# A third bank for the scores at the end of an attention kernel, and its last maxima one slot earlier

## What is computed

```python
x_n = _group_norm(x, gn_w, gn_b)
q, k, v = to_heads(conv1x1(x_n, wq, bq)), ...        # 4 images, 4 heads, 1024 pixels, 64
attn = jnp.einsum('bhqd,bhkd->bhqk', q, k) * scale
attn = jax.nn.softmax(attn, axis=-1)
out = jnp.einsum('bhqk,bhkd->bhqd', attn, v)
return x + conv1x1(out, wp, bp)
```

## Time and profile before

| | |
|---|---|
| median of 3 runs | 367.43 us (366.38 to 367.86) |
| the profiled execution's own time | 366.56 us |
| its span, first to last instruction | 364.8 us |
| mean granted TensorE clock | 0.998 |
| PE busy | 348.0 us, 95% |
| ACT busy | 303.1 us, 83% |
| DVE busy | 284.0 us, 78% |
| POOL busy | 284.2 us, 78% |

### The profile page before, as it was taken

The page is one execution under the profiler, slowest core; times in us unless marked ns, Lnnn a source line. Parts: engine busy times, 40 slices in busy tenths (PEclk is TensorE's granted clock), DMA queues, the critical chain, the costliest instruction groups (busy, mean ns, idle before and its releaser), DMA issues.

```text
span 364.8 us, 11244 instructions
## 1 busy us (share of the span) xinstructions
PE 348.0 (95%) x4577; PEld 208.6 (57%) x4577; DVE 284.0 (78%) x447; ACT 303.1 (83%) x362; POOL 284.2 (78%) x258
## 2 busy tenths in 40 slices
PE   0899999999999999999999999999999999999996
PEld 0544565655656556655666556565656556655564
DVE  5788899878887787778887777777877787787474
ACT  1748879898877999989878999998889888888982
POOL 5066888699788997998778997998879797967722
PEclk9999999999999999999999999999999999999999
DMA  6055141213743341143553241031552441070113
GB/s 212 19 146 144 45 97 38 30 62 103 135 142 74 80 98 43 24 112 116 124 154 66 60 106 64 10 80 43 117 164 53 94 85 65 2 202 3 31 31 118
DMA packets 38587, 30.92 MB, mean 85 GB/s; under 512 B 23676, under 2 KB 31368, under 8 KB 38536
## 3 DMA queue, kind: packets, MB, share of 16 engines
q1 hardware_dynamic: 37792, 29.15, 32.6%
q10 hardware_dynamic: 744, 1.06, 0.8%
HBM read 9.44 MB, written 4.19 MB: 37 GB/s over the span
## 4 chain that ended last, share of the span: by engine, by line
PE 85%; DVE 8%; ACT 2%; issue 2%; DMA 1%; DVEq 1%; ACTq 0%
PE gen L617 19%; PE st L743 14%; PE st L744 14%; PE pv L766 9%; PE pv L769 8%; PE pv L768 7%; PE st L709 5%; PE mx L709 3%; DVE mx L1053 3%; DVE p_lo L1086 2%; ACT st L969 1%; DVE mx L1049 1%; PE st L617 1%; PE mx L824 1%; DMA xin<-in_x_dram 1%
## 5 line engine op out<-in xcount | busy, mean ns | idle before, releaser
L964 ACT ACTIVATE p_hi<-st 128x1024 f16<-128x1024 f32 x127 | 130.7, 1029 | 40.2 <-PE st L744 38.8
L1328 POOL TENSOR_TENSOR p_lo<-p,p_hi 128x1024 f16<-128x1024 f32 x62 | 132.3, 2133 | 10.4 <-ACT p L969 10.4
L766 PEld LDWEIGHTS pv<-v_hi,p_hi 128*128 128x128 f16 x1024 | 93.4, 97 | 26.7 <-issue 15.0
L766 PE MATMUL pv<-v_hi,p_hi 128*128 128x65 f16 x1024 | 106.4, 195 | 0.3 <-DVE o L1094 0.2
L768 PE MATMUL pv<-v_lo,p_hi 128*128 128x64 f16 x1024 | 105.9, 193 | 0.0
L769 PE MATMUL pv<-v_hi,p_lo 128*128 128x65 f16 x1024 | 105.7, 194 | 0.0
L1086 DVE TENSOR_TENSOR p_lo<-st,p_hi 128x512 f16<-128x512 f32 x126 | 80.8, 683 | 30.0 <-ACT st L969 29.7
L743 PE MATMUL st<-q_twice,k_both 128*128 128x512 f16 x256 | 97.0, 379 | 1.6 <-DVE p_lo L1086 1.2
L768 PEld LDWEIGHTS pv<-v_lo,p_hi 128*128 128x128 f16 x1024 | 93.8, 98 | 6.2
L744 PE MATMUL st<-q_max,k_one 65*128 65x512 f16 x256 | 97.3, 380 | 0.0
L769 PEld LDWEIGHTS pv<-v_hi,p_lo 128*128 128x128 f16 x1024 | 93.9, 97 | 0.0
(11 more groups left out here) (200 smaller groups left out, 558.4 us busy)
## 6 DMA issues: line engine op xcount, KB each, us to landing
q_twice<-st_hi_q SPq DMA_DIRECT2D x64, 64.0 KB, 2.1
xres<-in_x_dram SPq DMA_DIRECT2D x4, 1024.0 KB, 5.2
out_dram<-y SPq DMA_DIRECT2D x13, 256.0 KB, 2.3
xin<-in_x_dram SPq DMA_DIRECT2D x6, 512.0 KB, 4.6
k_both<-st_hi_k SPq DMA_DIRECT2D x16, 128.0 KB, 2.3
k_one<-st_hi_k SPq DMA_DIRECT2D x16, 128.0 KB, 2.6
q_max<-st_lo_q SPq DMA_DIRECT2D x32, 64.0 KB, 2.1
k_both<-st_lo_k SPq DMA_DIRECT2D x16, 128.0 KB, 2.3
```

The costliest lines, as they stand in the source:

```text
L766: nc.tensor.matmul(pv_v[:, q, :], hi, vh, start=k == 0 and q == 0, stop=False, skip_group_check=True)
L964: nc.scalar.activation(p_hi[:, G % PR, :, :], scores, ACT.Exp, scale=SM_SCALE / M_SCALE)
L1328: nc.gpsimd.tensor_tensor(p_lo[:, G % PR, :, :], p_full(G), p_hi[:, G % PR, :, :], ALU.subtract)\
```

## The change

Three things, all in the last 18 slots. First, from slot 120 (`TRIPLE`) on the scores take turns in three double banks, mx, st0 and st1, instead of two: mx is free by then, since the last maxima are over. So scores of slot G wait for the reader of slot G - 3 instead of G - 2; slot 120 itself waits for the last shift. Second, the last pair of heads makes two of its maxima in slot 110, number 0 in st1 and number 1 in mx, and one in each of the slots 111 to 116; number 1 is reduced one slot later, in slot 111 of DVE, ahead of number 2. Third, since mx is no longer free for an output tile, the second of the two output tiles goes to the first bank of st1, and all six of its matmuls stand at the end; the first part in slot 123 is gone. The banks of the closing part change accordingly.

```diff
+    TRIPLE = TOTAL - 8
...
-        tail_banks = [st[0][:, 0:512], st[0][:, 512:1024], st[1][:, 0:512], st[1][:, 512:1024]]
-        last_banks = [gen, mxb[0]]
+        tail_banks = [st[0][:, 0:512], st[0][:, 512:1024], st[1][:, 512:1024], mxb[0]]
+        last_banks = [gen, st[1][:, 0:512]]
...
             if V == LAST_PAIR:
-                return [("two", V, m)]
+                return [("two", V, n) for n in ((0, 1) if m == 0 else (m + 1,)) if n < 2 * SPU]
...
-            return m in FIRST_IN_SCORES if V == SINGLES // 2 else V < LAST_PAIR and m % 2 == 0
+            return m in FIRST_IN_SCORES if V == SINGLES // 2 else m == 0 or V < LAST_PAIR and m % 2 == 0
...
-            return kind == "two" and SINGLES // 2 < n < LAST_PAIR and m % 2 == 1
+            return kind == "two" and (SINGLES // 2 < n < LAST_PAIR and m % 2 == 1 or (n, m) == (LAST_PAIR, 1))
...
-            return [item for item in maxima_at(G) if not one_slot_later(*item)] + \
-                   [item for item in pair_maxima(G - 1) if one_slot_later(*item)]
+            return [item for item in pair_maxima(G - 1) if one_slot_later(*item)] + \
+                   [item for item in maxima_at(G) if not one_slot_later(*item)]
...
+        def scores_bank(G):
+            return st[G % 2] if G < TRIPLE else (mx, st[0], st[1])[(G - TRIPLE) % 3]
+
+        def bank_user(G):
+            return G - 2 if G < TRIPLE else G - 3
...
-            tile = st[G % 2][:, :] if in_place(G) else p32[:, G // 2 % PB if G else PB - 1, :]
+            tile = scores_bank(G)[:, :] if in_place(G) else p32[:, G // 2 % PB if G else PB - 1, :]
...
-                if G > 1 and not in_place(G - 2):
-                    wait(pe, s_exp, G - 1)
+                if G == TRIPLE:
+                    wait(pe, s_mx_free, len(in_order))
+                elif G > 1 and not in_place(bank_user(G)):
+                    wait(pe, s_exp, bank_user(G) + 1)
...
-                    if G > 1 and in_place(G - 2):
-                        wait_p_lo(pe, G - 2, c)
+                    if G > 1 and G != TRIPLE and in_place(bank_user(G)):
+                        wait_p_lo(pe, bank_user(G), c)
...
-                    dst = st[G % 2][:, c * HALF:(c + 1) * HALF]
+                    dst = scores_bank(G)[:, c * HALF:(c + 1) * HALF]
...
-                if G in (TOTAL - 6, TOTAL - 5):
-                    i = G - TOTAL + 6
-                    wait(pe, s_mx_free, len(in_order))
-                    job("y", i, 0, B - 1, last_banks[i], only=0)
+                if G == TOTAL - 6:
+                    job("y", 0, 0, B - 1, last_banks[0], only=0)
...
-            job("y", 1, 0, B - 1, last_banks[1], only=1)
+            job("y", 1, 0, B - 1, last_banks[1])
...
-                scores = st[G % 2][:, :].rearrange("p (c n) -> p c n", n=HALF)
+                scores = scores_bank(G)[:, :].rearrange("p (c n) -> p c n", n=HALF)
```

## The result

| | before | change |
|---|---|---|
| median of 10 runs each, same chip | 366.90 us (365.96 to 367.86) | 368.84 us (367.15 to 370.06) |
| ratio, 95% interval | | 1.0055 [1.0038, 1.0072] |
| profiled execution | 366.56 us | 367.89 us |
| its span, mean granted clock | 364.8 us, 0.998 | 366.1 us, 0.995 |
| PE busy | 348.0 us | 348.0 us |

What follows compares the result with a forecast made beforehand. PE was taken as nearly full, waiting in a ring with ScalarE and VectorE through PSUM banks. 1.75 - 0.90 + 0.65 = +1.50 us, added to the three-run median 367.43, gave 368.9 us, range 367.0 to 370.3.

Steps and rivals of the forecast that it cites:

- The sum of +1.50: Whole change: 1.75 us stall in slot 111, less 0.90 regained by weighing 120, plus 0.65 for the late output tile.
- Slot 111: PE waits before pair 2 until VectorE, behind p_lo 110, has reduced pair 1; slot 112 starts 1.75 us late.
- Slots 118 to 124: Third bank ends the wait before scores 120; weighings 116 and 120 wait for normalisation; weighing 120 is 0.85 us late.
- Rival A: Slots 118 to 122 regain nothing, as first weighings hold PE for the normalisation: +2.40 us, 369.8; chance 0.22.
- rival B: Normalisation never holds PE, so the third bank pays for the stall: +0.44 us, 367.9; chance 0.08.
- The tile: The last output tile's first half leaves slot 123 for between weighings 125 and 126: +0.65 us, bounds 0 to 0.65.
- the 0.90 regained: By weighing 120, 0.90 of the 1.75 us delay is won back, leaving it 0.85 us late.
- The pair that leaves slot 117: Slot 117 without a pair frees some 0.3 us of PE, but behind that slot's scores; not counted in the sum.
- Rival D: The new pause in slot 111 halves PE's clock behind it: up to 4.2 us more, 373.1 at most; chance 0.04.

Runs made afterwards that it cites:

- the second kernel: The change with the maxima as before, keeping the third bank and the late output tile: 365.74 us, ratio 0.9975 to the kernel before.
- the first: The change with pair 1 reduced in slot 110, right behind pair 0 and ahead of p_lo 110: 365.79 us, ratio 0.9976 to the kernel before.

## Why the prediction was right, and where it was not

**The time.** 368.84 against 368.9. The sum of +1.50 in the trace is answered by +1.37 in the stretch: 0.80 late at weighing 120 (forecast 0.85), and 0.57 more from there to the end of the last weighing (forecast 0.65). That the medians agree to 0.1 us is luck. Two things that the sum left out, the clock and the closing stores, work against each other, and the medians of one series differ by 1.94, 0.44 more than the sum. And the forecast counted from the median of three runs, 367.43, which is 0.53 above that of ten, 366.90. The two errors nearly cancel.

**Slot 111.** Right: 1.75 us were forecast from rows of DVE's queue, the row shows 1.73, slot 112 at 323.27 (forecast 323.26). The kernel with pair 1 reduced at once shows the cause.

**Slots 118 to 124.** Right in mechanism and size, but for one attribution below. Scores 120 don't wait; weighing 116 comes at 341.02 (forecast 341.03), weighing 120 at 348.58 (forecast 348.63). Rival A (nothing regained) would have had the latter after 349.0; rival B (no wait of the normalisation) is refuted by the two rows of 0.82 and 0.32 us. The rule of the Trainium skill, "Perfetto Trace Analysis", section "Optimization Strategy", that a repeated bubble can mean too little PSUM for the next tile, is borne out only in part: the bank took the bubble before scores 120 away, and one of 0.82 us came up before the next matmul, until DVE's order was changed.

**The tile.** The sum's split was not clean. The forecast of +0.65 at the end contains 0.65 that had left slot 123, which it had credited to the bank as part of the 0.90 regained. Bank and tile together were -0.25 in the sum and measure -0.19; the tile by itself measures +0.18.

**The pair that leaves slot 117.** The forecast said that it frees PE only behind the scores of slot 117, and put it at nothing. But its sum gave ScalarE 1.86 us from the start of slot 117 to that of slot 118, where the trace of before has 2.04 (333.52 to 335.56), and booked the 0.18 to the bank. The traces show that they go with the pair: ScalarE takes 2.03 to 2.04 us there in the five traces with a pair in slot 117, the two with the third bank among them, and 1.82 to 1.83 in the seven without, the one with the old banks among them. So the right time of weighing 116 contains some 0.2 us that the pair gives and not the bank; the second kernel against the first has 41.64 - 41.41 = 0.23 for it.

**The clock.** This is the step that failed. Rival D had a chance of 0.04 and a price of up to 4.2 us. In place of that, kernels with the pause have 1.21 - 0.32 = 0.9 more falls per execution than those without, so by the mean clocks most executions have it, though of the four traces only one does; and the price is 1.53 us in that trace, not 4.2, since only slot 112 and most of the weighing ahead of it run at the lower level: slot 113 begins with 0.38 us a matmul again. That is about 0.9 x 1.5 = 1.4 us in the mean, an estimate. The forecast took a pause of 1.23 us near the start, without harm, as evidence against D. But one execution's row was none: the same pause stands in all twelve traces, and in four of them PE falls to the lower level 2.1 to 2.5 us after it has restarted. In the change's first trace:

```profile
17.33 0.59 PE L831 MATMUL mx<-st_hi_k,st_hi_q 64*128 64x512 f16 x2 [1.23 <-ACT st_hi_k L943]
...
20.03 0.63 PE L624 MATMUL st<-z_lo,w_hi_k 128*128 128x512 f16 x1
```

That this pause brings that fall was not tested. The Trainium skill, "TensorE: Matmul & The Clock Gate", section "HAM oscillation — how this bites in real kernels", says that the clock falls where a gap between groups of products is long enough; the gaps of its case are waits of some 3 to 5 us for a DMA. Here the fall follows a shorter wait, of 1.73 us, in the second trace of the change; in the first, with the same wait, there is none.

**The closing stores.** Also left out, and against the clock: from the end of the last weighing to the issue of the last two stores on ACT's queue the kernel before and the change take the same (3.51 and 3.50 us), but the stores land later in the kernel before. The DMA issues at the end of its second trace, and below them those of the change (queue, KB each, median us from issue to landing):

```profile
out_dram<-y SPq DMA_DIRECT2D x2, 128.0 KB, 2.3
out_dram<-y ACTq DMA_DIRECT2D x2, 128.0 KB, 2.6
```

```profile
out_dram<-y SPq DMA_DIRECT2D x2, 128.0 KB, 1.9
out_dram<-y ACTq DMA_DIRECT2D x2, 128.0 KB, 2.0
```

From the last weighing to the end of the span it is 7.13 and 7.52 us in the two traces of before, and 6.52 to 6.71 in the ten others. That gives back 0.4 to 1.0 us in every other kernel, and would explain why the tile alone is faster in the runs though its stretch is 0.18 longer. The executions bear it out: among those without a fall, the mean of each of the six other kernels without the pause, or with it filled, is 0.46 to 0.81 us lower, against that of the kernel before in the same series, than the stretches say; that of the kernel before, timed again, by 0.09. Why the stores land later in the kernel before stays open. The closing code is not enough for it: the second part alone, on the kernel before, has that code unchanged and ends in 6.60 us. Taken together, +1.37 in the stretch, -0.4 to -1.0 at the stores and +1.4 by the clock make +1.8 to +2.4; the medians of the same series differ by 1.94.

## What to carry to other kernels

Before a buffer is given a new writer, look where its reader stands in the other engine's in-order queue: here one place in VectorE's list was worth 1.79 us, and a bank added for PE brought most of its gain only when VectorE's normalisation stood ahead of its p_lo. When a change puts a new pause on PE, price two things: the pause itself, and a fall of the clock behind it; and count both over several executions, since one trace may show no fall where others do. A single row in which a pause went by unharmed is no evidence that it always does. Moving work from one place of a full engine to another is to be booked at both places at once, or its gain and its cost land in different terms.

## What was not expected of the hardware

The clock fell not in the pause but after it: in the second trace of the change pair 2 starts at 322.41, the weighing behind it has its usual 0.19 us a matmul until 323.58, and from 323.61 on the matmuls grow longer, so some 1.2 us after PE has restarted.

```profile
323.58 0.19 PE L778 MATMUL pv<-v_hi,p_lo 128*128 128x65 f16 x1
...
323.64 0.23 PE L777 MATMUL pv<-v_lo,p_hi 128*128 128x64 f16 x1
```

With zero products in the pause the stretch behind it stays at 1.00 in the trace, and no execution of that kernel is in the cluster of two falls. And a fall happens in some executions of one and the same program and not in others: by the mean clock, in 27 of 71 of the kernel before, and wherever a trace shows one away from the pause of slot 111, it is near the start, at 19.5 to 23.5 us. What decides it stays open.
